# A windowed-attention and ternary-FFN layer: weight preparation moved from a stage of its own into the pipeline, and PV issued once per head group

## The chip, the cores and the metric

One core of a Trainium2 chip runs the kernel. The metric is the device time of one execution in microseconds.

## The reference

Input x is (8, 1024, 512) in fp32. Two sublayers follow each other, each with a layer norm ahead of it and one behind it, inside the residual:

```
x = x + layernorm(attn(layernorm(x)))
x = x + layernorm(ffn(layernorm(x)))

attn: q, k, v = x @ W.T + b; 16 heads of 32; blocks of 256 queries see the 256 keys
      up to and with their own; softmax; out @ Wo.T + bo
ffn:  h = x @ tern(w_fc).T + gate * (x @ v.T @ fast_b.T @ u.T)
      r = relu(h); out = (r * r) @ tern(w_proj).T
tern(w) = clip(round(w / s), -1, 1) * s,  s = mean(|w|) of each row (at least 1e-5)
```

w_fc is (2048, 512), w_proj (512, 2048), the four attention weights (512, 512), u (2048, 16), v (16, 512).

## The kernel before

All operands of products are split into an fp16 part and an fp16 rest (`product3` multiplies three of the four combinations), scaled by powers of two, so that an fp32-like result comes out of fp16 matmuls. The weights therefore need work before use: their largest absolute value (for the power of two), the two parts, a transpose; for the FFN the mean of absolute values of each row, a ternary value for every element, a transpose.

`build` runs two stages, each a block of its own with its own memory. **`prepare`** does all weight work: it loads Wq, Wk, Wv, Wo (1 MB each) and eight pieces of 1 MB of w_fc and w_proj, takes maxima on VectorE and across partitions with GpSimd's `partition_all_reduce`, splits on ScalarE and VectorE (L406, L471), sums absolute values on ScalarE (L422), makes the ternary values on VectorE (L493, L496), transposes everything 128 by 128 on TensorE (L377, L383, L390, L396), which VectorE and ScalarE copy out of PSUM (L350), and computes some 40 small constants on VectorE (L508 to L557).

**`steps`** then loops over 32 steps of 256 rows (4 a sequence, `t` the step, `p = t % 4` its place). Each step has 32 slots, one for each of 4 head groups x 2 query tiles x 4 heads, and five engines run the same slot program, written out by hand: tables such as `QK_SLOT` or `FF1_SLOT` say at which slot a piece of work is issued and lags (`LAG_T`, `LAG_PV`) how many slots a consumer comes after. `due(it, table, slot, lag, base)` gives the entries that fall on a slot, for the step `base` ahead of or behind the one whose scores are running. Projections are made one to two steps ahead, x is normalized two to three steps ahead, output projection and FFN run one to two steps behind; so the loop runs from -2 to 34. An engine goes through its items in order; a semaphore wait of one item holds all behind it.

In a step, scores S of a head are made on TensorE (L740), masked with a row maximum on VectorE (L1027), exponentiated on ScalarE for the row sum (L910); then the scores are made a second time transposed, T (L754), with the shift inside the product, exponentiated straight into `PT` (L924), masked on GpSimd (L1236, L1239), and multiplied with V on TensorE (L771, `Ob`): four heads of a group side by side in 128x32 column tiles, in fp32. `weighted_values` is called for each half (past keys, own keys) of a head group, two batches of 16 matmul records per group; a sequence's first step has only the second half. `PT` has 8 buffers.

SyncE's queue issues all DMAs: the loads of x, the transposes of the normalized x (`turn_x` L653, `turn_x2` L664, 128x1024 fp16 each), the transposes of the softmax shift (L676) and, for each head group, 12 DMAs that stack the parts of q and k on partitions (`stack`, L691). `qk32` has two buffers; the FFN's output tile `yc` is separate from the attention's `yb`.

## Time and profile before

| | us |
|---|---|
| median of 3 runs (2378.79 to 2380.89) | 2378.9 |
| profiled execution | 2378.28 |
| its span, first to last instruction | 2376.6 |
| TensorE busy in it | 2217.4 |
| VectorE busy | 1696.3 |
| ScalarE busy | 1643.4 |
| GpSimd busy | 1355.0 |

The span is that of one execution taken by the profiler; what lies around it is 1.7 us. "Busy" of TensorE counts from a matmul's start to its modelled end, and matmuls overlap. SPq is SyncE's queue, whose rows are the times it takes to issue DMAs. PEclk is the granted clock as a share of full speed. DMA share is the mean busy share of the 16 DMA engines.

### The profile page before, as it was taken

How to read it: one execution, taken by the hardware profiler on the slowest of the kernel's cores; microseconds unless marked ns; L12 is line 12 of the kernel's file. 1: busy time of each engine (PE TensorE's matmuls, PEld its weight loads, DVE VectorE, ACT ScalarE, POOL GpSimd, SP SyncE). 2: the span in 40 equal slices, each digit the busy share in tenths (PEclk: the TensorE clock that was granted, in tenths of full speed). 3: DMA queues.
4: the chain of work that ended last, by engine and by line, in shares of the span. 5: the costliest groups of instructions: out<-in, count | busy, mean ns of one | idle time of the engine just before them, and what ended most of it. 6: DMA issues, size and time to landing. Idle time of an engine off the chain costs nothing.

```text
span 2376.6 us, 60643 instructions
## 1 busy us (share of the span) xinstructions
PE 2217.4 (93%) x20124; PEld 1645.5 (69%) x20124; DVE 1696.3 (71%) x4247; ACT 1643.4 (69%) x4613; POOL 1355.0 (57%) x2473
## 2 busy tenths in 40 slices
PE   3267899999999999999999999999999999999998
PEld 2244677777777777777777777777777777777665
DVE  7535677777777777777777777777777777777754
ACT  4326777677767777677766777677776777677762
POOL 2023566566656666666665666665665666655553
PEclk9588999999999999999999999999999999999999
DMA  6112223322223222222222232232222322232210
GB/s 224 27 44 69 59 62 72 76 70 61 63 69 72 60 68 73 73 62 71 60 66 69 66 74 63 71 71 62 63 64 74 73 70 60 73 67 53 59 30 27
DMA packets 323336, 159.90 MB, mean 67 GB/s; under 512 B 203456, under 2 KB 293568, under 8 KB 322512
## 3 DMA queue, kind: packets, MB, share of 16 engines
q1 hardware_dynamic: 323024, 156.03, 26.7%
q8 instruction: 161, 2.64, 0.5%
q14 instruction: 151, 1.24, 0.2%
HBM read 46.83 MB, written 16.78 MB: 27 GB/s over the span
## 4 chain that ended last, share of the span: by engine, by line
PE 82%; SPq 5%; DMA 3%; ACT 2%; DVE 2%; issue 1%; POOL 0%; POOLq 0%; ACTq 0%; DVEq 0%
PE Ab L781 19%; PE F L836 19%; PE F L863 15%; PE Cb L781 9%; PE Ob L771 7%; PE Tb L754 6%; PE S L740 5%; SPq L691 5%; PE F L848 3%; DMA x2T<-xs 2%; DMA xT<-xs 1%; ACT PT L924 1%; ACT Sm L910 0%; DVE lnst L1044 0%; DVE Sm L1027 0%
## 5 line engine op out<-in xcount | busy, mean ns | idle before, releaser
L924 ACT ACTIVATE PT<-Tb 128x384 f32<-128x384 f32 x896 | 438.8, 490 | 418.9 <-PE Tb L754 413.7
L910 ACT ACTIVATE Sm<-Sm,nmax 128x384 f32<-128x384 f32 (+2 forms) x1024 | 584.2, 571 | 129.7 <-DVE nmax L1027 126.1
L1027 DVE CUSTOM_DVE_ANT_0 Sm<-S,mask,scales 128x384 f32<-128x384 f32 (+2 forms) x1024 | 572.2, 563 | 120.6 <-PE S L740 109.9
L836 PE MATMUL F<-x2T,t 128*128 128x256 f16 x4096 | 489.1, 272 | 0.0
L863 PE MATMUL F<-t,r 128*128 128x512 f16 x2048 | 483.5, 379 | 0.7 <-DVE r L1129 0.7
L836 PEld LDWEIGHTS F<-x2T,t 128*128 128x128 f16 x4096 | 397.9, 98 | 52.2
L781 PE MATMUL Ab<-xT,w_attn 128*128 128x256 f16 x3072 | 384.5, 276 | 37.0 <-DMA xT<-xs 32.3
L781 PEld LDWEIGHTS Ab<-xT,w_attn 128*128 128x128 f16 x3072 | 294.0, 99 | 95.5 <-issue 49.3
L1239 POOL TENSOR_SCALAR_AFFINE_SELECT PT<-PT 128x256 f32<-128x256 f32 x512 | 260.8, 513 | 173.5 <-ACT PT L924 172.7
L863 PEld LDWEIGHTS F<-t,r 128*128 128x128 f16 x2048 | 195.5, 98 | 201.0 <-ACT r L974 4.6
L740 PE MATMUL S<-QK 96*128 96x384 f16 (+2 forms) x1280 | 315.4, 280 | 10.3 <-DVE nmax L1027 10.3
L1256 POOL TENSOR_TENSOR sq<-r 128x512 f32<-128x512 f32 x256 | 272.5, 1064 | 81.1 <-ACT r L974 79.3
L754 PE MATMUL Tb<-QK 128*128 128x256 f16 (+1 forms) x1792 | 295.5, 247 | 23.5 <-ACT PT L924 21.5
L1208 POOL TENSOR_TENSOR lnrs<-lnve,nhalf 128x1 f32<-128x1 f32 x256 | 166.7, 651 | 173.8 <-DVE lnve L1099 60.3
L1236 POOL TENSOR_SCALAR_AFFINE_SELECT PT<-PT 128x256 f32<-128x256 f32 x384 | 184.9, 482 | 134.0 <-ACT PT L924 132.1
L754 PEld LDWEIGHTS Tb<-QK 128*128 128x128 f16 x1792 | 170.8, 98 | 102.3 <-ACT PT L924 28.7
L1129 DVE TENSOR_TENSOR r<-sq,r 128x512 f16<-128x512 f32 x256 | 188.5, 737 | 57.1 <-POOL sq L1256 29.3
L974 ACT ACTIVATE r<-F,c 128x256 f32<-128x256 f32 x512 | 211.8, 467 | 15.8 <-PE F L848 13.9
L1244 POOL TENSOR_TENSOR qkp<-qk,qkp 128x512 f16<-128x512 f32 x128 | 159.3, 1245 | 72.6 <-DVE qkp L1076 72.6
L781 PE MATMUL Ab<-w_attn,xT 128*128 128x256 f16 x1536 | 189.2, 273 | 9.5 <-ACT qk L948 9.5
L910 ACT ACTIVATION_READ_ACCUMULATOR Sm<-Sm,nmax 128x1 f32 x1024 | 197.9, 193 | 0.0
L771 PE MATMUL Ob<-PT,V 128*32 128x128 f32 (+1 forms) x3584 | 194.1, 334 | 0.0
(158 smaller groups left out, 3007.7 us busy)
## 6 DMA issues: line engine op xcount, KB each, us to landing
QK<-qkp SPq DMA_DIRECT2D x1536, 32.0 KB, 1.9
xa<-in_x SPq DMA_DIRECT2D x64, 256.0 KB, 2.9
x<-in_x SPq DMA_DIRECT2D x64, 256.0 KB, 3.0
out<-yc SPq DMA_DIRECT2D x64, 256.0 KB, 2.2
stage<-in_w_fc SPq DMA_DIRECT2D x4, 1024.0 KB, 9.2
stage<-in_w_proj SPq DMA_DIRECT2D x4, 1024.0 KB, 5.8
turned<-parts SPq DMA_TRANSPOSE x128, 2.3
stage<-in_Wq SPq DMA_DIRECT2D x1, 1024.0 KB, 5.5
```

Source lines behind the costliest of these rows:

```text
L740: mm = pe.matmul(Sb[j % 2][:, place * P:(place + n) * P], Q3[0:ST, h, qc * P:(qc + 1) * P], K3[0:ST, h, slot * P:(slot + n) * P], start=Tr ...
L754: mm = pe.matmul(Tb[:, col:col + width], K3[:, h, ring + key:ring + key + P], Q3[:, h, q0:q0 + width], start=True, stop=True, skip_group_c ...
L771: mm = pe.matmul(Ob[r * HD:(r + 1) * HD, q0:q0 + width], V[:, c, h * HD:(h + 1) * HD], src[:, blk * P:blk * P + width], start=(first and k ...
L781: mm = pe.matmul(outp, a(pa, k), b(pb, k), start=(n == 0), stop=(n == 3 * KD - 1), skip_group_check=True)
L836: pe.matmul(Fb[b][:, half * STEP:(half + 1) * STEP], W["t1"][:, k, mc * P:(mc + 1) * P], x2T[:, part, k, :], start=(half == 0 and k == 0 a ...
L863: mm = pe.matmul(o[:, :], r2[:, part, m, i * P:(i + 1) * P], W["t2"][:, m, :], start=(m == 0 and part == 0), stop=(m == KH - 1 and part == 1),
L910: act.activation(blk, blk, ACT.Exp, bias=nmax[:, hg % 2, j % 8:j % 8 + 1], scale=-1.0, accum_out=sums[:, hg % 2, j % 8:j % 8 + 1]).then_in ...
L924: act.activation(PT[:, n % NPT].rearrange("p b n -> p (b n)"), Tb[:, 0:WIN], ACT.Exp, bias=1.0, scale=c_score).then_inc(M["T_exp"], 1)
L974: ins = act.activation(r32[:, b, half * STEP:(half + 1) * STEP], Fb[b][:, half * STEP:(half + 1) * STEP], ACT.Relu, scale=W["c1"][:, 2 * m ...
L1027: v.tensor_tensor_reduce(Sm[:, j % NSM, c0:WIN], Sb[j % 2][:, c0:WIN], W["mask"][:, c0:WIN], W["c"][:, 3:4], 3e38, ALU.add, ALU.min, nmax[ ...
L1239: g.affine_select(out=blk, in_=blk, compare_op=ALU.is_ge, fill=zero, base=0, pattern=[[0, 2], [1, P]], channel_multiplier=-1).then_inc(M[" ...
L1256: g.tensor_tensor(sq32[:, m % 2], r32[:, m % 2], r32[:, m % 2], ALU.mult).then_inc(M["r2_sq"], 1)
```

## The change

`prepare` is gone; there is one block. What it did goes to three places.

At the head, ahead of the slot loop (`weights()` on each engine): loads of Wq and Wk, then x of step 0; their maxima, which no longer go through GpSimd: TensorE transposes the column of 128 partial maxima, broadcast, into PSUM (`turn_columns`), and VectorE reduces it (`read_columns`); the split; the transposes of Wq and Wk as DMAs from SyncE (four of 128x1024 each, `turn_weight`), then `turn_x` of step 0.

In the slots of the first steps, as items (`prologue(it, table, slot, lag)`, which counts slots from the loop's begin, 64 being the first slot of step 0): Wv at 24 and Wo at 44; the eight FFN pieces at 50, 58, ... 106, each over 12 slots (abs sums on ScalarE, comparison on GpSimd, ternary step on VectorE, DMA transposes by SyncE at lag 11: four of 128x512 for w_fc, one of 128x2048 for w_proj); the constants at 82 to 114. ScalarE's queue issues the loads of the pieces. Their buffers lie in tiles that the loop doesn't use yet.

In every step: `weighted_values` runs once for a head group with all four spans (32 records; 16 in a sequence's first step); `PT` has 12 buffers counted through all steps; `qk32` has one buffer; `yc` is `yb`.

```diff
+PIECES = 8
+WEIGHT_SLOT = {24: 2, 44: 3}
+PIECE_SLOT = {50 + 8 * n: n for n in range(PIECES)}
+PIECE_LOAD = {34: 2, 50: 3, 64: 4, 72: 5, 96: 6, 104: 7}
+CONST_SLOT = {82: 0, 85: 1, 87: 2, 88: 3, 89: 4, 90: 5, 112: 6, 114: 7}
...
+def prologue(it, table, slot, lag):
+    entry = table.get((it.t - BEGIN) * SLOTS + slot - lag)
+    if entry is not None:
+        yield entry
...
-        qk32 = sb("qk32", [P, 2, 2, STEP], F32)
+        qk32 = sb("qk32", [P, 2, STEP], F32)
-        NSM, NPT = 3, 8
+        NSM, NPT = 3, 12
-        yc = sb("yc", [P, TILES, D], F32)
+        yc = yb
...
+            def turn_weight(w):
+                sp.wait_ge(M["w_lo"], w + 1)
+                for c in range(KD):
+                    sp.dma_start(W["w"][:, w, :, :, c * P:(c + 1) * P].rearrange("p a k n -> p (a k) n"),
+                                 w_split[w][:, c].rearrange("p a i -> p (a i)"),
+                                 transpose=True).then_inc(M[f"w_turned{w}"], 16)
+            def turn_piece(n):
+                sp.wait_ge(M["f_tern"], n + 1)
+                if n < 4:
+                    for m in range(4):
+                        sp.dma_start(W["t1"][:, :, (4 * n + m) * P:(4 * n + m + 1) * P],
+                                     f_tern[n % 2][:, m * D:(m + 1) * D],
+                                     transpose=True).then_inc(M[f"f_turned{n % 2}"], 16)
+                else:
+                    sp.dma_start(W["t2"][:, :, (n - 4) * P:(n - 3) * P], f_tern[n % 2],
+                                 transpose=True).then_inc(M[f"f_turned{n % 2}"], 16)
...
+                    for w in prologue(it, WEIGHT_SLOT, s, 4):
+                        turn_weight(w)
+                    for n in prologue(it, PIECE_SLOT, s, 11):
+                        turn_piece(n)
...
+            def turn_columns(k, cols):
+                pe.wait_ge(M["col_max"], k + 1)
+                need(pe, M["max_read"], k)
+                for j, c in enumerate(cols):
+                    mm = pe.transpose(Fb[0][:, j * P:(j + 1) * P], c.to_broadcast([P, P]), idf)
+                mm.then_inc(M["turned_max"], 1)
...
-            def weighted_values(t, p, hg, half):
-                n = tile_of(p, 8 * hg + half * GROUP + GROUP - 1)[3]
-                pe.wait_ge(M["T_masked"], tiles_before(t, p) + n + 1)
+            def weighted_values(t, p, hg):
+                last = tile_of(p, 8 * hg + 2 * GROUP - 1)[3]
+                pe.wait_ge(M["T_masked"], tiles_before(t, p) + last + 1)
+                need(pe, M["OT_lo"], t * NGROUP + hg)
                 pe.wait_ge(M["A_free"], t * NA + V_POS[1] + 1)
+                now, past = p * TILES, (p - 1) * TILES
+                spans = [(now, 0, 0, STEP, 0), (now + 1, 2, P, P, 0)]
+                if p:
+                    spans = [(past + 1, 1, 0, STEP, GROUP), (past, 0, 0, P, GROUP)] + spans
...
-                    if ok and i % GROUP == GROUP - 1 and tile_of(p, i):
-                        weighted_values(t, p, i // 8, i // GROUP % 2)
+                    if ok and i % 8 == 7:
+                        weighted_values(t, p, i // 8)
...
+                weight_hi(0)
+                weight_hi(1)
+                for i in range(TILES):
+                    a_hi(0, i)
+                for n in range(2):
+                    act.wait_ge(M[f"w_turned{n}"], KD * 16)
+                    load_piece(n)
...
+            def output_max():
+                then(v.tensor_tensor(u_sc, u_in, u_in, ALU.mult))
+                then(v.tensor_reduce(usq, u_sc, AX.X, ALU.add))
+                v.tensor_reduce(red[:, 7:8], usq, AX.X, ALU.max)
+                weight_max(3, 6).then_inc(M["col_max"], 1)
```

## Rows read from the trace of the kernel before

**Rows 1.** Windows by stage: stretch, length, busy us (instructions) of each engine, PEclk, DMA share, GB/s.

```profile
0.00:116.00 116.00, 30.65 (x285) 27.64 (x286) 76.92 (x161) 50.11 (x71) 15.42 (x43) 0.71 0.38 125
116.00:139.60 23.60, 19.07 (x144) 14.62 (x144) 6.16 (x14) 3.04 (x8) 4.48 (x5) 0.90 0.05 19
139.60:180.80 41.20, 22.46 (x170) 17.36 (x170) 14.74 (x55) 15.23 (x54) 9.13 (x20) 0.83 0.27 66
180.80:229.90 49.10, 34.08 (x292) 23.16 (x292) 28.04 (x88) 33.42 (x107) 18.88 (x50) 0.86 0.25 60
229.90:293.40 63.50, 52.72 (x516) 39.05 (x514) 43.64 (x110) 44.59 (x129) 31.34 (x70) 0.95 0.27 64
...
363.20:2225.00 1861.80, 1853.51 (x16989) 1381.90 (x16987) 1392.01 (x3511) 1363.89 (x3899) 1155.76 (x2083) 1.00 0.28 67
```

**Rows 2.** Timeline of the weight stage: start us, us, engine, line, operation.

```profile
4.43 9.02 POOL L296 CAST QK<-ksel 32x512 f16<-32x512 f32 x16
6.31 2.29 DVE L449 TENSOR_REDUCE red<-stage 128x1 f32<-128x2048 f32 x1 [6.31 <-DMA stage<-in_Wq]
...
25.84 7.68 ACT L406 ACTIVATE s_hi<-stage,sW 128x2048 f16<-128x2048 f32 x4 [23.78 <-DVE sW L467]
27.88 6.88 DVE L471 SCALAR_TENSOR_TENSOR s_lo<-stage,sW,s_hi 128x2048 f16<-128x2048 f32 x3 [1.19 <-ACT s_hi L406]
...
57.25 0.62 ACT L422 ACTIVATE junk<-stage 128x512 f16<-128x512 f32 x1
59.16 1.67 DVE L493 TENSOR_SCALAR s_lo<-stage,h 128x512 f16<-128x512 f32 x4
60.87 2.74 DVE L496 SCALAR_TENSOR_TENSOR s_hi<-stage,h,s_lo 128x512 f16<-128x512 f32 x4
...
89.17 0.15 DVE L514 TENSOR_SCALAR bnd<-pow_out 128x1 f32<-128x1 f32 x1 [7.18 <-POOL pow_out L306]
...
96.07 0.91 DVE L557 COPY u_stack<-u_part 128x256 bf16<-128x256 bf16 x6
```

**Rows 3.** Timeline from the first x to the first projection.

```profile
108.06 5.93 SPq L653 DMA_TRANSPOSE xT<-xs  x2
...
115.94 5.15 PE L781 MATMUL Ab<-xT,w_attn 128*128 128x256 f16 x24 [16.91 <-DMA xT<-xs]
```

**Rows 4.** Timeline of SyncE's queue in the fill.

```profile
140.98 7.81 SPq L691 DMA_DIRECT2D QK<-qkp  x12
...
180.85 1.24 SPq L653 DMA_TRANSPOSE xT<-xs  x1
```

**Rows 5.** SyncE's waits, from 139.6 to 180.8, then from 180.8 to 229.9.

```profile
SPq L674 <- POOL parts L1228: 1.1, 1, 1.1
...
SPq L81 <- PE Tb L754: 4.7, 3, 2.6
SPq L81 <- POOL parts L1228: 3.3, 2, 2.1
```

**Rows 6.** Windows: weight loads, and the second xT transpose (columns as above).

```profile
20.00:40.00 20.00, 8.15 (x84) 7.79 (x85) 18.03 (x24) 13.80 (x17) 0.72 (x2) 1.00 0.75 276
...
113.80:115.94 2.14, 0.00 (x0) 0.03 (x1) 0.00 (x0) 0.00 (x0) 0.00 (x0) 0.50 0.78 153
```

**Rows 7.** Timeline of TensorE around one PV batch; PV's records from 363 to 2225.

```profile
1039.57 0.33 PE L754 MATMUL Tb<-QK 128*128 128x256 f16 x2
1039.74 0.33 PE L740 MATMUL S<-QK 96*128 96x384 f16 x1
1040.00 0.86 PE L771 MATMUL Ob<-PT,V 128*32 128x256 f32 x16
1040.79 0.39 PE L848 MATMUL F<-z,u_T 96*128 96x256 bf16 x2
...
L771 PE MATMUL Ob<-PT,V x3072: 272/326/404, 365.7 to 2221.0; 128*32 128x256 f32 x192
```

**Rows 8.** Timeline: GpSimd's rest of one head group, ScalarE's next write of qk32.

```profile
999.99 1.16 POOL L1244 TENSOR_TENSOR qkp<-qk,qkp 128x512 f16<-128x512 f32 x1 [0.88 <-DVE qkp L1076]
...
1006.31 0.46 ACT L946 ACTIVATE qk<-Ab,bqs 128x256 f32<-128x256 f32 x1
```

More of the change, by code:

```diff
@@ new lines, in steps, with carve @@
+        f_raw = [w_raw[n] if n in (2, 3) else r2w.bitcast(F32)[:, n % 2 * 4 * D:(n % 2 + 1) * 4 * D] for n in range(PIECES)]
+        f_junk = V[:, 6:8].rearrange("p c d -> p (c d)").bitcast(F16)
+        f_below = r32[:].rearrange("p a n -> p (a n)").bitcast(F16)
+        f_tern = [sq32[:].rearrange("p a n -> p (a n)").bitcast(F16), x2T[:].rearrange("p a k n -> p (a k n)")]
+        u_stack = V[:, 4:6].rearrange("p c d -> p (c d)").bitcast(BF16).rearrange("p (m c) -> p m c", m=KH)
+        def carve(tile, widths):
+            flat, at, out = tile, 0, []
+            for w in widths:
+                out.append(flat[:, at:at + w])
+                at += w
+            return out
@@ L724, in _, with weights, low_rank_weights, output_scales @@
         def _(pe):
+            def turn_columns(k, cols):
[4 more added lines that the diff above has]
+                mm.then_inc(M["turned_max"], 1)
+            def weights():
+                pe.wait_ge(M["pool_ready"], 2)
+                turn_columns(0, [red[:, 0:1]])
+                turn_columns(1, [red[:, c:c + 1] for c in range(1, 4)])
+            def low_rank_weights():
+                pe.wait_ge(M["fb6_done"], 1)
+                pe.wait_ge(M["max_read"], 4)
+                for k in range(KD):
+                    mm = pe.matmul(Fb[0][:, k * LR:(k + 1) * LR], v_in[:, k * P:(k + 1) * P], fb6, start=True, stop=True)
+                mm.then_inc(M["vp_full"], 1)
+            def output_scales():
+                pe.wait_ge(M["s2_ready"], 1)
+                pe.wait_ge(M["max_read"], 5)
+                for c in range(KD):
+                    mm = pe.transpose(Fb[0][:, c * P:(c + 1) * P], s2c[:, c:c + 1].to_broadcast([P, P]), idf)
+                mm.then_inc(M["s2_full"], 1)
             def scores(t, p, j):
@@ L892, in body @@
                         scores_transposed(t, p, i)
+            weights()
             run_iterations(pe, body)
@@ L1012, in body @@
                         z_second(t)
+            weights()
             run_iterations(act, body)
@@ L1198, in body @@
                         masked_scores(it.t, it.p, s)
+                    for w in prologue(it, WEIGHT_SLOT, s, 0):
+                        value_max() if w == 2 else output_max()
+                    for w in prologue(it, WEIGHT_SLOT, s, 1):
+                        value_scale() if w == 2 else output_scale()
+                    for w in prologue(it, WEIGHT_SLOT, s, 3):
+                        weight_lo(w)
+                    for n in prologue(it, PIECE_SLOT, s, 4):
+                        thresholds(n)
+                    for q in range(4):
+                        for n in prologue(it, PIECE_SLOT, s, 5 + q):
+                            ternary(n, q)
+                    for k in prologue(it, CONST_SLOT, s, 0):
+                        ffn_consts(k)
+            weights()
             run_iterations(v, body)
@@ L1290, in body @@
                             second_residual(t, p, i)
+            weights()
             run_iterations(g, body)
```

769 lines of the change are left out of this document (372 added, 397 removed).

## The prediction

> **What bounds the kernel now.** I read the execution by stages first, cutting it where SyncE issues the transpose of the next step's x [rows 1]. The last row of that group is the steady state: TensorE is busy 1853.5 of 1861.8 us, at full clock. Nothing taken from VectorE, ScalarE, GpSimd or the queues pays there; only TensorE's own time does. The first row is the opposite: `prepare` and the first x take 116 us with TensorE busy 30.7 us, and nothing in it is attention. The three rows after it are the fill of the pipeline: 23.6, 41.2 and 49.1 us, TensorE busy 19.1, 22.5 and 34.1 us. So I read those two places apart: what stands on the way to the first projection, and what paces the fill. In the fill that is SyncE's queue. Twelve stacking DMAs take 7.8 us to issue [rows 4], a step has 48 of them, and in the first 41.2 us stretch SyncE, once it has begun, waits only 1.1 us, in the next 4.7 + 3.3 = 8.0 us [rows 5]. In the steady state the same 30 us of issue hide under a step of some 68 us (1861.8 us hold 27.4 steps).
>
> Times below are sums against the profiled execution, 2378.28 us for a span of 2376.6; the median of the runs, 2378.9, lies 0.6 above.
>
> **The head.** Before, the first projection matmul starts at 115.94, behind three matters: all weight work (its last constants end at 97.0 [rows 2], two copies follow), then the load of x and its statistics, then its two transposes [rows 3]. After, only Wq and Wk stand in front. I walk the new chain on rows of the same shapes [rows 2]. Wq is there at 6.3; its maximum takes 2.29 (8.6). The transpose through TensorE and the read of 128 columns replace GpSimd's all-reduce; the trace has no such pair, so I take two semaphore hops and a small reduce, 1 us, between 0.5 and 2 (9.6). Three small VectorE operations of 0.2 give the scale (10.2). The fp16 part of a weight costs ScalarE 7.68/4 = 1.92, the rest 6.88/3 = 2.3 on VectorE. VectorE does in order: maximum of Wk (12.8), its columns and scale (15), statistics of x tile 0 (16), the rest of Wq (18.4), x again, the rest of Wk (22.5), x (25), constants (27). The 4.5 MB in front, at the 276 GB/s of a stretch full of such loads [rows 6], take some 16 us and are in by 18, when SyncE's queue is wanted for the first transpose.
>
> From 18.4 the DMA engines set the pace: four transposes of Wq, four of Wk, two of x, each of 128x1024 fp16 as the xT transpose of now. That one keeps the 16 engines 78% busy over 2.14 us, which is 1.67 us of all of them [rows 3, 6] and more than the 1.24 of its issue [rows 4]. Ten take 16.7, and 1.5 us pass before the first moves: 36.6. ScalarE starts the loads of two FFN pieces behind the transposes of Wq and Wk, 1 MB each, on the same engines; at 276 GB/s that is 3.8 us a piece, of which about one falls in front of x. First projection: 40, between 35 (loads hidden, everything as above) and 48 (both loads in front and the constants late). Change **-76** (-81 to -68).
>
> A page speaks about this rate. The Trainium skill ("DMA: Bandwidth & Descriptors", section "Latency and other measured facts") gives a DMA transpose 261 GB/s; 256 KB would then take 1.0 us, ten 10 us, and the head would be some 7 us shorter. The trace shows 256 KB in 1.67 us, which is 157 GB/s, and the sum above goes by that.
>
> **From there to the first stretch's cut** (23.6 us before). The projections of step 0 are TensorE's, 19.1 of 23.6 us, so what comes between counts. Wv's split and transposes run while the four Q/K halves do and just arrive (estimate 51 for a use at 51): nothing, up to 4 if late. Wo's maximum is a wait put into TensorE's order: the four column transposes stand between the halves of V tile 1 and the last Q/K group, and wait for VectorE's two 0.42 us passes over u and a 2.29 us maximum, 3.5 in all, less the half of V already queued: +3. Then SyncE waits for Wo's rest and issues its four transposes before x of step 1, 4 x 1.67 us of engine time in front of it: +5 on top of a cut that must in any case wait for the last projection (xT is one buffer). FFN pieces 2 and 3 loading beside it: +2. Together **+10** (5 to 18).
>
> **First filled stretch** (41.2 us before, SyncE without slack). Pieces 0, 1 and 2 are turned in it, four transposes each; twelve issues of 1.24 are 15, less the 1.1 us of wait and another 1 from the stacking rows that now wait less: **+13** (8 to 20). What the other engines get: four abs sums of 0.62 per piece on ScalarE (2.5 us); the ternary step, four of 0.69, on VectorE; the comparison on GpSimd, which the trace prices on VectorE at 0.42 and for a GpSimd pass of 512 elements at 9.02/16 = 0.56 [rows 2], so 2.2 us a piece, at most twice that. Three pieces are 8, 9 and 7 to 14 us on engines that are busy 15.2, 14.7 and 9.1 of 41.2 [rows 1]: covered.
>
> **Second filled stretch** (49.1 us before, 8.0 us of SyncE wait). Piece 3 (four issues), pieces 4 to 6 and u (one each, of 128x2048, twice the engine time of xT's): eight issues, 10 us, less 8: +2. The low-rank constants, which now run from 89.17 to 96.97 as one chain on VectorE [rows 2], fall into seven slots together with ternary steps; VectorE is busy 28.0 of 49.1 and gets 8 + 11 more, which fits over the stretch but not over those slots: +4. **+6** (0 to 18). The last piece and the s2 rows fall into a stretch of 63.5 us in which SyncE has room: nothing, up to 3. If this cover failed, late FFN weights would hold `turn_x2` of step 0 and SyncE behind it.
>
> **PV once per head group.** The matmuls are the same, the batches fewer: 4 x 7 x 8 = 224 become 128; 96 times an entry and an exit go. A batch of 16 records starts 0.26 after the S matmul before it, which itself streams 0.17 (T to S in the same rows), and the next operation starts 0.79 later [rows 7]. Four heads run side by side, so it streams twice 256 and twice 128 columns. A record lasts 0.272 at 128 columns and, half of them being twice as wide with the middle at 0.326, about 0.38 and at most 0.404 at 256; so 128 columns stream in 0.107 to 0.13, and six such units in some 0.64. So 0.26 - 0.17 + 0.79 - 0.64 = 0.24 us of a batch is entry and exit. 96 x 0.24 = 23; some of it falls into the fill, and a batch twice as long holds S and T back once, so I take **-20** (-23 to 0).
>
> The Trainium skill ("TensorE: Matmul & The Clock Gate", section "Measured speedup vs the span model") has packed tiles cost one matmul's time and about 4 ns a tile more. By that a batch has next to no entry of its own, and joining them saves at most a few us, not 20. The 0.24 us above is what this trace shows.
>
> **At nothing.** `qk32` with one buffer: ScalarE's next write must wait for GpSimd's rest of the group before; that one starts at 999.99, takes 1.16, and the next write starts at 1006.31 [rows 8]: 5 us of cover. If it went, TensorE would wait at Ab. `yc` in `yb`'s place: VectorE's own order puts the last read of yb tile 0 one slot ahead of the write, and the store leaves ten slots (20 us) before its reuse. PT's twelve buffers: a tile is reused two slots after its batch, as before. The end of the kernel is as it was.
>
> **Sum:** -76 + 10 + 13 + 6 - 20 = -67, thus 2311; I add 3 for small waits in the third stretch: **2314**.
>
> **Rivals.**
> 1. Forecast, 2314, own range 2300 to 2330: chance 0.58.
> 2. The items choke the fill: VectorE and ScalarE, not SyncE, become its pace because the items come in bursts and in an in-order queue. Each of the two stretches then takes its high end and the head its high end: -68 + 18 + 20 + 18 - 20 = -32: 2346. For: a slot of the fill lasts 1.3 to 1.5 us and an item adds 0.8 to it on each of three engines, with waits from one to the other. Against: the busy times above. 0.14.
> 3. Joining PV saves nothing, because TensorE then waits for T's exponentials, or because the 0.24 us isn't paid per batch: 2334. Against: TensorE's records are gapless otherwise. 0.14. The span model of the Trainium skill named above would end here too.
> 4. Transposes queued back to back go at the pace of their issue, 1.24 instead of 1.67 us: ten are 4.3 us shorter, 2310, and perhaps a little more from Wo's and the pieces': 2307. Against: 256 KB were never moved faster than in the row. 0.06. The Trainium skill's rate for DMA transposes leads to the same place.
> 5. Slower than before: the joined batch stalls TensorE at every group, all steps long, since it needs the masks of eight tiles and holds S and T. All but PV gives -47; over 128 groups that is used up at 0.37 us each. At 0.5 it would be 2378 - 47 + 64 = 2395. For: it is the only edit that acts in the steady state, where all counts. Against: the second half batch already waited for the same last mask at the same lag. 0.04.
> 6. The change doesn't do what it says: FFN weights come so late that the head only moves, and step 0's FFN waits for what was saved: around 2378. Against: the last piece is turned ten slots before its first use. 0.04.
>
> The range reaches from just below case 4 to part of case 2: 2294 to 2342. A change under 0.2% (4.8 us) can't be told from none here. Faster 0.94 (cases 1 to 4 and part of 6), same 0.02, slower 0.04.
>
> **What would show it.** The first projection near 40, ten transposes before it back to back; the three cuts 34, 54 and 55 us apart instead of 23.6, 41.2 and 49.1; SyncE without wait in the first two; 32 records per PV batch with one gap at either side, and the step time in the steady state 0.7 us lower in three of four. Wrong: the first projection later than 50; an FFN wait of TensorE in step 0; waits of ScalarE at `qk` or VectorE at `yb` in every step.

## The result

The changed kernel takes **2346.68 us** (median of four runs, 2345.23 to 2347.89) against 2378.85 for the kernel before, measured beside it: a ratio of 0.9865, 95% interval 0.9848 to 0.9882. The sign was right, the forecast of 2314.0 was 33 us too low, and the range, which ended at 2342.0, missed the time by 4.7 us. The profiled run took 2345.23 us for a span of 2343.5.

Windows of the changed kernel, cut as [rows 1] were, with the columns of that group: the head, then from the first projection on to the cuts where SyncE issues the transpose of the next step's x, and the steady state.

```profile
0.00:54.00 54.00, 9.47 (x54) 6.50 (x54) 25.41 (x51) 10.22 (x10) 19.48 (x39) 0.99 0.88 236
54.00:82.50 28.50, 14.07 (x98) 10.45 (x98) 11.33 (x21) 5.42 (x10) 2.98 (x3) 0.80 0.25 65
82.50:138.30 55.80, 27.58 (x177) 19.19 (x177) 30.32 (x81) 25.49 (x86) 33.29 (x33) 0.74 0.46 120
138.30:208.20 69.90, 42.18 (x300) 26.79 (x301) 52.41 (x158) 41.77 (x133) 47.94 (x68) 0.74 0.47 110
208.20:274.00 65.80, 55.45 (x514) 41.17 (x513) 44.53 (x112) 44.79 (x129) 33.00 (x73) 0.87 0.31 69
...
343.60:2192.00 1848.40, 1836.76 (x16988) 1388.22 (x16986) 1385.96 (x3512) 1365.77 (x3900) 1165.37 (x2084) 1.00 0.27 68
```

And the timeline rows that set the cuts (the first is TensorE's first projection):

```profile
41.73 4.66 PE L540 MATMUL Ab<-xT,w_attn 128*128 128x256 f16 x24 [11.50 <-DMA xT<-V]
...
82.55 1.25 SPq L313 DMA_TRANSPOSE xT<-xs  x1
...
138.29 1.24 SPq L313 DMA_TRANSPOSE xT<-xs  x1
...
208.19 1.24 SPq L313 DMA_TRANSPOSE xT<-xs  x1
...
274.00 1.24 SPq L313 DMA_TRANSPOSE xT<-xs  x1
```

With the same rows of before (115.94, 139.64, 180.85, 229.87, 293.37) every term of the prediction's sum gets its measured size:

| stretch | before | after | change | predicted |
|---|---|---|---|---|
| start to the first projection | 115.9 | 41.7 | -74.2 | -76 |
| to the first cut | 23.7 | 40.8 | +17.1 | +10 (5 to 18) |
| first filled stretch | 41.2 | 55.7 | +14.6 | +13 (8 to 20) |
| second | 49.0 | 69.9 | +20.9 | +6 (0 to 18) |
| third | 63.5 | 65.8 | +2.3 | +3 |
| the rest, to the end | 2083.2 | 2069.5 | -13.7 | -20 (-23 to 0) |
| span | 2376.6 | 2343.5 | -33.1 | -64 |

The head came close to its working. Three terms did not: the way to the first cut (7 us), the second filled stretch (15 us) and PV (6 us). Stretches are read from one profiled execution of each kernel and scatter more than the medians do: over the fifteen kernels of this document that join PV "the rest" lies between 2069.3 and 2074.9, and the changed kernel's 2069.5 is at its low end, so PV's gain by this reading is 8 to 14 us. In the windows the second stretch has VectorE busy 52.4 us where it was 28.0 before, GpSimd 47.9 for 18.9, and TensorE's granted clock at 0.74 for 0.86; yet the busiest of them, VectorE, fills only three quarters of it. The experiments ask what set its length.

**PV.** TensorE's timeline around one joined batch of a steady step; the matmul behind it starts where the next row does:

```profile
1108.91 0.33 PE L496 MATMUL S<-QK 96*128 96x128 f16 x2
1109.17 1.51 PE L530 MATMUL Ob<-PT,V 128*32 128x256 f32 x32
1110.61 0.61 PE L540 MATMUL Ab<-xT,w_attn 128*128 128x256 f16 x4
```

From the last start of S to the next operation are 0.26 + 1.44 = 1.70 us for 32 records. Two batches of 16 took, by [rows 7], 2 x (0.26 + 0.79) less one S matmul of 0.17, that is 1.93. A joined batch saves 0.23 us, as the prediction's 0.24 had it.

**What SyncE did.** Its waits in the first and second filled stretch:

```profile
SPq L340 <- DVE sq L991: 1.0, 1, 1.0
SPq L87 <- POOL parts L1325: 0.2, 1, 0.2
...
SPq L87 <- POOL parts L1325: 7.0, 2, 4.0
SPq L87 <- PE Tb L512: 3.6, 2, 3.4
SPq L423 <- DVE V L1040: 3.4, 1, 3.4
```

In the first it waits 1.2 us of 55.8: there the queue is full, as forecast. In the second it waits 14.0 us, against 8.0 before [rows 5], and half of that for the row sums at the end of the attention work. The prediction had these waits used up by eight more issues; they grew instead. So the second stretch isn't SyncE's.

### The profile page after: what moved, and what is told of

It is laid out like the page before. It is cut to its first block, busy times and chain, and to the rows that moved or that the text cites. A ratio compares the mean times of both kernels' runs of the same rounds, so it can differ in the third digit from the quotient of the medians.

```text
span 2343.5 us, 60162 instructions
## 1 busy us (share of the span) xinstructions
PE 2188.6 (93%) x19862; PEld 1635.4 (70%) x19862; DVE 1685.0 (72%) x4242; ACT 1626.6 (69%) x4613; POOL 1422.9 (61%) x2499
## 4 chain that ended last, share of the span: by engine, by line
PE 74%; DVE 8%; SPq 6%; issue 4%; ACT 3%; DMA 2%; POOL 1%; ACTq 0%; DVEq 0%; POOLq 0%
PE Ab L540 18%; PE F L608 17%; PE F L635 11%; PE Cb L540 9%; PE Ob L530 6%; PE Tb L512 6%; PE S L496 5%; SPq L401 3%; PE F L620 2%; DVE lnst L1073 1%; DMA x2T<-xs 1%; DVE QK L1065 1%; DVE yb L1124 1%; SPq L331 1%; ACT Sm L731 1%
## 5 line engine op out<-in xcount | busy, mean ns | idle before, releaser
L540 PE MATMUL Ab<-xT,w_attn 128*128 128x256 f16 x3072 | 385.4, 276 | 40.8 <-DMA xT<-xs 23.7
L1336 POOL TENSOR_SCALAR_AFFINE_SELECT PT<-PT 128x256 f32<-128x256 f32 x512 | 267.2, 527 | 111.3 <-ACT PT L750 107.6
L1257 POOL TENSOR_TENSOR lnrs<-lnve,nhalf 128x1 f32<-128x1 f32 x256 | 174.8, 683 | 165.0 <-DVE lnve L1131 60.2
L1333 POOL TENSOR_SCALAR_AFFINE_SELECT PT<-PT 128x256 f32<-128x256 f32 x384 | 186.3, 485 | 129.1 <-ACT PT L750 127.4
L1161 DVE TENSOR_TENSOR r<-sq,r 128x512 f16<-128x512 f32 x256 | 188.7, 738 | 56.5 <-POOL sq L1353 28.8
L540 PE MATMUL Ab<-w_attn,xT 128*128 128x256 f16 x1536 | 199.5, 282 | 19.7 <-ACT qk L776 14.7
L1314 POOL TENSOR_TENSOR shift_c<-sums,isum 128x8 f32<-128x8 f32 x128 | 28.6, 223 | 284.8 <-ACT isum L739 284.8
```

Of the source, the lines that this page charges most:

```text
L540: mm = pe.matmul(outp, a(pa, k), b(pb, k), start=(n == 0), stop=(n == 3 * KD - 1), skip_group_check=True)
L1161: v.tensor_tensor(lo, sq32[:, m % 2], hi, ALU.subtract).then_inc(M["r2_lo"], 1)
L1336: g.affine_select(out=blk, in_=blk, compare_op=ALU.is_ge, fill=zero, base=0, pattern=[[0, 2], [1, P]], channel_multiplier=-1).then_inc(M[" ...
```

## The experiments

Each is the changed kernel with one edit unless it says otherwise. Medians of four runs; the ratio is to the kernel before, measured beside each (2378.66 to 2378.99). "Lengths" are the stretches of the table above, from the first projection: to the first cut, first, second and third filled stretch (changed kernel: 40.8, 55.7, 69.9, 65.8). Ten kernels leave the way to the first cut as it is (the changed one; comparison moved or left out, single transposes, PV halves, constants, sooner loads; the three with added work). They reach it after 38.1 to 42.4 us, so 4 us of that length come and go by themselves. In the kernels whose edit leaves them alone, the first filled stretch takes 55.6 to 56.5 us, the second 69.5 to 69.9.

### The comparison on VectorE, and left out

The comparison of the ternary step was priced at 0.56 us, twice that at most. The groups of the changed kernel say (count, busy us, mean ns, idle before):

```profile
L1266 POOL TENSOR_SCALAR r<-r,yb 128x512 f16<-128x512 f32 x24 | 38.9, 1629 | 22.0 <-DVE yb L981 22.0
L1266 POOL TENSOR_SCALAR r<-t,yb 128x512 f16<-128x512 f32 x8 | 12.4, 1562 | 4.6 <-DVE yb L981 4.6
```

That is 1.6 us each, 51 us in all. The first kernel does the comparison on VectorE in front of each ternary operation; the second leaves it out, so that its FFN weights aren't the ternary ones.

```diff
-                    for q in range(4):
-                        for n in prologue(it, PIECE_SLOT, s, 4 + q):
-                            below(n, q)
...
+                v.tensor_scalar(f_below[:, cols], f_raw[n][:, cols], h[:, 0, c:c + 1], None,
+                                ALU.is_lt).then_inc(M["f_below"], 1)
                 v.wait_ge(M["f_below"], 4 * n + q + 1)
```

> The changed kernel with the FFN pieces' comparison (32 operations of 128x512, 1.56 us each on GpSimd in the trace after) moved to VectorE, where the same shape took 0.42 us. Theory G (GpSimd's comparisons pace the two filled stretches, because VectorE's ternary step waits for each and masks and q/k rests queue behind them): 15 to 25 us faster than the changed kernel, 2322 to 2332, both stretches shorter. Theory S (SyncE's transposes pace them): at most 3 us, 2344 to 2347. Theory V (VectorE is the pace, with its constants): slower by up to 10 us, since VectorE gets 13 us more.

> The changed kernel with the comparison left out altogether (the ternary step subtracts the raw weight in its place, so FFN values are not the reference's). It bounds what the comparison can cost wherever it runs. G: 18 to 28 us faster than the changed kernel, a few us more than with VectorE doing it. S: at most 3. V: as with the comparison on GpSimd.

On VectorE: **2341.10** (2340.73 to 2342.15), 0.9840 [0.9823, 0.9856]; lengths 42.1, 55.6, 66.1, 65.4. Left out: **2339.59** (2339.11 to 2342.40), 0.9838 [0.9822, 0.9854]; lengths 40.0, 55.3, 65.3, 65.9. The same operation costs VectorE 0.51 us (groups of the first kernel):

```profile
L990 DVE TENSOR_SCALAR r<-r,yb 128x512 f16<-128x512 f32 x24 | 12.3, 511 | 0.0
```

GpSimd loses some 22 to 26 us of work in each of the two stretches (33.3 to 10.7 and 47.9 to 21.9 us by the windows), and the first gets no shorter, the second by 3.8 to 4.6. So the whole comparison, at 1.6 us apiece on GpSimd, is worth 5.6 to 7.1 us of the time, not more: theory G, with its 15 to 28, is out, and S and V, which allowed no gain of this size, don't hold either.

The two kernels also price VectorE's time. Their windows of the first and second stretch, with the comparison on VectorE, then left out:

```profile
83.60:139.20 55.60, 27.12 (x181) 19.58 (x182) 36.42 (x103) 25.82 (x87) 10.73 (x21) 0.78 0.46 120
139.20:205.30 66.10, 39.55 (x291) 24.76 (x289) 53.78 (x166) 40.60 (x128) 21.85 (x50) 0.74 0.48 116
```

```profile
81.70:137.00 55.30, 29.39 (x176) 20.67 (x177) 26.47 (x81) 22.71 (x77) 9.77 (x18) 0.69 0.47 120
137.00:202.30 65.30, 40.64 (x296) 26.11 (x297) 49.65 (x161) 43.37 (x140) 22.36 (x52) 0.75 0.52 118
```

VectorE has 10.0 and 4.1 us less to do in the second kernel, 14.1 together, and the stretches are 0.3 and 0.8 us shorter, 1.1 together, no more than their scatter. And while GpSimd does the comparison, VectorE's own ternary operations take longer: 32 of them 29.8 us in the changed kernel, 24.8 with the comparison on VectorE.

### ScalarE's second load, and the loads beside the transposes

The chain from the first projection to the first cut in the changed kernel, timeline:

```profile
26.48 10.19 ACTq L712 DMA_DIRECT2D r<-in_w_fc  x2
...
31.10 0.17 DVE L889 RECIPROCAL yb<-yb 128x1 f32<-128x1 f32 x1
...
38.66 2.00 ACT L687 ACTIVATE PT<-t,yb 128x2048 f16<-128x2048 f32 x1 [14.17 <-issue]
...
54.05 5.30 PE L540 MATMUL Ab<-w_attn,xT 128*128 128x256 f16 x24 [3.92 <-DMA w_attn<-PT]
...
69.79 2.00 ACT L687 ACTIVATE PT<-t,yb 128x2048 f16<-128x2048 f32 x1 [5.89 <-DVE yb L889]
...
74.21 0.37 ACTq L712 DMA_DIRECT2D t<-in_w_fc  x1
74.21 8.24 SPq L331 DMA_TRANSPOSE w_attn<-PT  x4
```

Wv's scale is ready at 31.3, and its split starts at 38.66, for ScalarE goes through its items in order: it first waits for Wk's transposes so as to start the second FFN load, done at 36.67, and then loads three registers. And both `load_piece(2)` and `(3)` wait for the same semaphore as the transposes of Wv and Wo, `w_lo`; a load of 1 MB and four transposes start at the same instant. Two kernels: the second load as an item at slot 30; loads 2 and 3 behind the transposes.

```diff
-                for n in range(2):
-                    act.wait_ge(M[f"w_turned{n}"], KD * 16)
-                    load_piece(n)
+                act.wait_ge(M["w_turned0"], KD * 16)
+                load_piece(0)
...
+                if n == 1:
+                    act.wait_ge(M["w_turned1"], KD * 16)
```

> The changed kernel, but ScalarE doesn't wait for Wk's transposes and load FFN piece 1 before it splits Wv; that wait and load come at count 30, after the split. In the trace after, Wv's scale is ready at 31.2 and its split starts at 38.66. Theory A (this order makes V's first tile late): V's projection starts at its place right behind the second q/k group, some 5 us earlier, Wo's chain and everything behind it too: 5 to 8 us faster than the changed kernel. Rival (the cut waits for the transposes of Wo, whose time is set by the DMA engines): at most 2 us.

**2341.47** (2339.46 to 2344.93), 0.9839 [0.9823, 0.9856]; lengths 35.2, 55.8, 69.6, 67.2. The first cut comes 5.6 us sooner after the first projection, and the median is 5.2 lower, at the low end of theory A's 5 to 8.

```diff
                 if n in (2, 3):
-                    act.wait_ge(M["w_lo"], n + 1)
+                    act.wait_ge(M[f"w_turned{n}"], KD * 16)
...
-PIECE_LOAD = {34: 2, 50: 3,
+PIECE_LOAD = {46: 2, 60: 3,
```

> The changed kernel with the loads of FFN pieces 2 and 3 behind the transposes of Wv and Wo (ScalarE waits for these before it issues them, at counts 46 and 60) instead of starting with them. In the trace after, the load of piece 3 and the first of Wo's transposes are issued at the same 74.21, SyncE's queue is held for 8.2 us by four transposes instead of 5.2, and the 16 engines are full until 84. Theory D (the loads hold the transposes on the shared engines): x of step 1 is turned 4 to 7 us earlier after the first projection, 4 to 7 us faster than the changed kernel. Rival (the loads only move, and the sums of their pieces wait): within 2 us.

**2339.53** (2337.90 to 2340.81), 0.9836 [0.9819, 0.9852]; lengths 32.2, 55.8, 69.5, 65.9. Wo's transposes now hold SyncE's queue 5.3 us instead of 8.2 and begin 5.8 us earlier (timeline):

```profile
68.37 5.30 SPq L331 DMA_TRANSPOSE w_attn<-PT  x4
73.78 1.25 SPq L313 DMA_TRANSPOSE xT<-xs  x1
```

The two edits remove the same wait, and with it a fall of TensorE's clock. In the changed kernel TensorE stands idle for 3.92 us before V's first tile, until Wv's transposes have landed, and then its 24 matmuls take 5.30 us, at a granted clock of 0.51 (window 54.05 to 59.35), the lower of the two levels. In either kernel of this section V starts at its place, with 0.97 us ahead of it, and takes 2.78 at full clock. The kernel with single transposes (next section) has the wait and not the fall, and reaches the cut in 38.1 us instead of 40.8 (timeline):

```profile
52.86 2.79 PE L538 MATMUL Ab<-w_attn,xT 128*128 128x256 f16 x24 [3.90 <-DMA w_attn<-PT]
```

So here is the +17.1 of the second term: some 3 us of it are the wait for Wv's transposes, which either edit takes away, 2.5 the clock behind it, which falls in some kernels and not in others, and 2.9 the load beside Wo's transposes, which only the second edit takes away. With both edits the way takes 32.7 us (below), no less than with the second alone; the 8.5 to 9 us that it is still longer than before are the size of the forecast's other two terms, Wo's maximum and Wo's transposes (+3 and +5).

### One transpose for a w_fc piece

`t1` is laid out so that a piece is one transpose of 128x2048 instead of four of 128x512 (`turn_piece`), 12 issues fewer.

```diff
-                    for m in range(4):
-                        sp.dma_start(W["t1"][:, :, (4 * n + m) * P:(4 * n + m + 1) * P],
-                                     f_tern[n % 2][:, m * D:(m + 1) * D],
-                                     transpose=True).then_inc(M[f"f_turned{n % 2}"], 16)
+                    sp.dma_start(W["t1"][:, 4 * n * KD * P:4 * (n + 1) * KD * P].rearrange("p (c n) -> p c n", n=P),
+                                 f_tern[n % 2], transpose=True).then_inc(M[f"f_turned{n % 2}"], 16)
```

> The changed kernel with t1 laid out so that each w_fc piece is turned by one DMA of 128x2048 instead of four of 128x512: 12 issues of 1.3 us fewer on SyncE (15.6 us), same bytes. S (SyncE's issues pace the filled stretches): 10 to 15 us faster than the changed kernel. G: 0 to 4 us.

**2340.83** (2340.20 to 2341.49), 0.9840 [0.9824, 0.9857]; lengths 38.1, 51.2, 70.1, 65.5. The three pieces turned in the first stretch hold SyncE 1.7, 3.2 and 1.7 us instead of 5.2 each, which frees 9 us; the stretch gets 4.5 shorter, the second, where a fourth piece is turned, not at all. That is what the waits said: SyncE counts in the first stretch alone, and even there at half its price. The median gained 5.9 us, between theory S and theory G; some 2.7 of the profiled run's gain is the clock on the way to the first cut (the section above).

### PV in two batches again

```diff
+                    if p and half != k // 2:
+                        continue
...
-                    if ok and i % 8 == 7:
-                        weighted_values(t, p, i // 8)
+                    if ok and i % GROUP == GROUP - 1 and tile_of(p, i):
+                        weighted_values(t, p, i // 8, i // GROUP % 2)
```

> The changed kernel with PV issued in two batches per head group again, at the slots where the kernel before issued them; twelve PT buffers, one qk32 buffer and yc in yb's place stay. It measures the joining alone. Theory P (entry and exit of a batch, 0.2 to 0.24 us, are paid on TensorE's path): 96 more of them, 13 to 23 us slower than the changed kernel, 2360 to 2369, with the same fill. Rival (the 14 us that the steps after the fill lost come from the other edits): 2345 to 2350.

**2355.92** (2352.66 to 2359.99), 0.9900 [0.9883, 0.9916]; lengths 42.4, 56.4, 69.9, 66.4: 9.2 us more in the median, less than the 13 to 23 of theory P. In its profiled run, the slowest of its four, there are 12.5 more behind the fourth cut (2082.0 for 2069.5), where it stands as the kernel before did (2083.2). It has the twelve PT buffers, the single `qk32` and `yc` in `yb`'s place, so these three together cost next to nothing there. The batch is again that of [rows 7]:

```profile
1040.16 0.33 PE L496 MATMUL S<-QK 96*128 96x384 f16 x1
1040.41 0.86 PE L533 MATMUL Ob<-PT,V 128*32 128x256 f32 x16
1041.20 0.50 PE L544 MATMUL Ab<-xT,w_attn 128*128 128x256 f16 x3
```

Joining is the cause of the gain in the steady state. It is smaller than 96 x 0.23 = 22. In a window with the same number of matmuls ([rows 1] and the last row of after, 16989 and 16988) TensorE is busy 16.75 us less, and idle 11.6 us for 8.3: 3.3 come back as waits. One wait of TensorE in that window grew, for the softmax shift that VectorE writes into `QK` for T:

```profile
PE Tb L512 <- DVE QK L1065: 5.8, 21, 0.9
```

It was 0.6 us, once, before, and in the kernel with halves it is 0.6 again: the longer batch brings it. The window holds 27 of 32 steps, so about 82 of the 96 joins; 16.75/82 is 0.20 each. The others lie mostly in the fill, where TensorE isn't the bound.

### Later constants, sooner loads

The forecast put the second stretch's cost partly on the low-rank constants, which fall into seven slots with ternary steps. One kernel spreads them; another starts the last two FFN loads four slots sooner, since ScalarE waits 3.8 us for them.

```diff
-CONST_SLOT = {82: 0, 85: 1, 87: 2, 88: 3, 89: 4, 90: 5, 112: 6, 114: 7}
+CONST_SLOT = {79: 0, 82: 1, 85: 2, 88: 3, 91: 4, 95: 5, 112: 6, 114: 7}
...
-PIECE_LOAD = {34: 2, 50: 3, 64: 4, 72: 5, 96: 6, 104: 7}
+PIECE_LOAD = {34: 2, 50: 3, 64: 4, 72: 5, 92: 6, 100: 7}
```

> The changed kernel with the constants' items at counts 79, 82, 85, 88, 91, 95 instead of 82, 85, 87, 88, 89, 90. In the trace after, VectorE is a closed chain from 147.7 to 159.3 in the second stretch, SyncE waits 3.4 us for its last link (u), and four step-0 stackings queue behind. Theory V (the burst holds S and SyncE): 4 to 8 us faster than the changed kernel, all in the second stretch. Rival (the same work costs the same wherever it lies on an in-order engine): within 2 us.

> The changed kernel with the loads of FFN pieces 6 and 7 issued at counts 92 and 100 instead of 96 and 104; their sums come at 98 and 106. In the trace after, ScalarE waits up to 3.2 us for such a load in the second stretch, and the chain shows 4.9 us of it. Theory L: 3 to 6 us faster than the changed kernel. Rival: the wait on the piece two before moves to ScalarE instead, within 1.5 us.

Spread: **2345.59** (2340.41 to 2347.59), 0.9859 [0.9843, 0.9875]; second stretch 68.0. Sooner: **2345.54** (2343.71 to 2349.95), 0.9866 [0.9849, 0.9882]; second stretch 70.6. Neither can be told from the changed kernel, as both rivals had it. In the second kernel ScalarE's 3.8 us of waits for loads are gone from the second stretch, and its waits for VectorE's maxima have grown from 11.5 to 17.1: a wait that the table of waits names can be taken away and another takes its place.

### Together, and the work of each engine made dearer

> Three of the edits at once: comparison on VectorE, load of piece 1 behind Wv's split, w_fc pieces turned by one DMA each; alone they gave 5.6, 5.2 and 5.9 us. If the stalls follow each other on one chain (theory C: the fill is a chain of hand-offs between in-order queues, with no engine as its pace), the gains add to 14 to 18 us: 2329 to 2333. If they all draw on the same slack (one pacing resource behind them), 2337 to 2341.

The comparison on VectorE, the later second load and the single transposes together: **2334.85** (2333.19 to 2336.88), 0.9814 [0.9797, 0.9830]; lengths 36.1, 51.6, 68.6, 65.4. Alone they gave 5.6, 5.2 and 5.9 us, 16.7 in sum; together 11.8, between the two theories. The way to the first cut and the first stretch keep their gains; the second stretch, 66.1 with the comparison on VectorE alone, is back at 68.6.

If one engine paced the second stretch, its work would count fully and that of the others not at all. So three kernels add work in the two stretches: each ternary operation of VectorE done twice, each abs sum of ScalarE twice, and four 512-column matmuls of TensorE into a spare bank in each slot.

```diff
+                then(v.scalar_tensor_tensor(f_tern[n % 2][:, cols], f_raw[n][:, cols], h[:, 1, c:c + 1],
+                                            f_below[:, cols], ALU.is_gt, ALU.subtract))
...
+                act.activation(f_junk[:, q * D:(q + 1) * D], f_raw[n][:, q * D:(q + 1) * D],
+                               ACT.Abs).then_inc(M["act_step"], 1)
+                act.wait_ge(M["act_step"], 4 * n + q + 1)
...
+                    if 50 <= (it.t - BEGIN) * SLOTS + s < 114:
+                        for _ in range(4):
+                            pe.matmul(Fb[1][:, :], fill[:, 0:P], fill[:, 0:512], start=True, stop=True,
+                                      skip_group_check=True)
```

> The changed kernel with each ternary operation on VectorE done twice (same result): 32 more of 0.69 us and a wait for the first, some 0.8 us each, 12 to 13 us more VectorE work in each filled stretch. Its slope says how far VectorE paces the fill. Theory V (VectorE, 52.4 of 69.9 us busy in the second stretch, is its pace): that stretch grows by 10 to 13 us, the first, 30.3 of 55.8 busy, by less than 5; in all 12 to 18 us slower than the changed kernel. Theory C (hand-offs between in-order queues, no single pace): a third to a half of the added time in either stretch, 8 to 12 us in all. If neither, under 4.

> The changed kernel with each abs sum on ScalarE done twice: 32 more of 0.62 us and a wait, some 0.7 us each, 11 us more in each stretch on an engine busy 25.5 of 55.8 and 41.8 of 69.9 us. V: under 5 us in all. C: a third to a half, 7 to 11 us in all.

> The changed kernel with four dummy matmuls of 128x512 (bf16, 0.21 us each at full clock) into an unused bank at the head of each slot from count 50 to 113, so that TensorE's granted clock, 0.74 in both filled stretches after against 0.83 and 0.86 before, stays higher. It adds 0.86 us a slot, 27 us a stretch, where TensorE had 28 us idle. Theory K (the lower clock lengthens every TensorE hop of the fill, 42.2 us busy instead of 34.1 for the same work): clock above 0.9 and the two stretches together unchanged or shorter in spite of the added work, -6 to +6 us. Rival (TensorE's clock lies off the path): the added work shows where it stands in front of S and T, 10 to 30 us slower.

Windows of the two stretches, VectorE's work doubled, then ScalarE's, then TensorE's filled up:

```profile
82.30:143.00 60.70, 28.30 (x177) 19.17 (x177) 41.55 (x96) 25.70 (x87) 36.64 (x33) 0.75 0.44 110
143.00:219.00 76.00, 43.83 (x283) 26.45 (x284) 63.13 (x172) 40.36 (x128) 53.67 (x69) 0.68 0.41 102
```

```profile
81.30:138.70 57.40, 28.89 (x177) 19.89 (x177) 31.03 (x81) 34.13 (x99) 33.34 (x33) 0.73 0.47 116
138.70:210.40 71.70, 42.33 (x287) 26.25 (x288) 53.22 (x157) 50.50 (x147) 47.52 (x68) 0.72 0.51 107
```

```profile
82.00:141.40 59.40, 43.28 (x273) 26.86 (x273) 31.66 (x85) 25.83 (x87) 34.75 (x36) 0.88 0.46 113
141.40:211.10 69.70, 59.66 (x420) 36.09 (x421) 51.66 (x155) 42.35 (x131) 46.39 (x64) 0.93 0.45 110
```

| doubled | us | ratio | work added, 1st / 2nd | length added, 1st / 2nd |
|---|---|---|---|---|
| VectorE | 2358.07 | 0.9914 [0.9897, 0.9930] | 11.2 / 10.7 | 5.0 / 6.1 |
| ScalarE | 2350.22 | 0.9883 [0.9866, 0.9900] | 8.6 / 8.7 | 1.6 / 1.8 |
| TensorE | 2349.77 | 0.9874 [0.9855, 0.9893] | 15.7 / 17.5 | 3.6 / -0.2 |

VectorE's added work counts by 0.45 and 0.57, ScalarE's by 0.2 (lengths little above the scatter), GpSimd's (taken away, above) by up to 0.18, SyncE's by half in the first stretch and nothing in the second. By the medians VectorE's doubling lies inside theory C's 8 to 12 us (11.4), ScalarE's (3.5) below C's 7 to 11 and where theory V had it. TensorE's added matmuls made the two stretches 3.4 us longer, within theory K's -6 to +6. TensorE's is free in the second stretch, at 60 us busy of 70: its low clock costs nothing there that I can see, since the clock rose from 0.74 to 0.93 with the added matmuls, and the length stayed. (Extra time and faster own work may also cancel; one kernel doesn't part them.)

A share belongs to the kernel in which it was taken, not to the engine. The doubled ternary operations stand behind GpSimd's slow comparison; with that comparison gone from GpSimd, VectorE doing it or nobody is 14.1 us of VectorE's time and counted 1.1, that is by 0.08. Why the two differ so was not tried. No engine's work counts fully, so none of them alone is the pace. That the pace is the way through all their queues is what is left, and the shares fit it; no run shows it directly.

### All edits

The next takes the three of before with the spread constants and the sooner loads; the one behind it adds the loads behind the transposes; the last divides the comparison between VectorE (first and third quarter of a piece) and GpSimd.

> Comparison on VectorE, load of piece 1 behind Wv's split, w_fc pieces turned by one DMA each, loads of pieces 6 and 7 sooner, constants spread. The first three gave 11.8 us together, the last two 1 us each alone. If VectorE's burst and the loads come to matter once the others are gone: 2326 to 2331. If not: 2332 to 2336.

> The five edits and the loads behind the transposes. D, and gains that follow each other on one chain: 3 to 6 us faster than the five, 2324 to 2327. If not, 2328 to 2331.

> As the six together, but of each piece's four comparisons two stay on GpSimd, two go to VectorE. Theory V (with all four, VectorE paces the second stretch): that stretch 1 to 4 us shorter, 1 to 4 us faster than the six. Rival (each hand-off between the two costs what it saves): same or up to 3 us slower.

| | us | ratio | lengths |
|---|---|---|---|
| five edits | 2329.74 (2328.28 to 2331.61) | 0.9797 [0.9781, 0.9813] | 35.1, 50.2, 62.2, 66.4 |
| six | 2326.24 (2322.20 to 2330.51) | 0.9782 [0.9764, 0.9800] | 32.7, 50.8, 61.4, 65.5 |
| six, comparison divided | 2325.94 (2323.83 to 2328.68) | 0.9784 [0.9768, 0.9801] | 32.2, 50.7, 60.6, 65.7 |

Constants and loads, worth some 1 us each when alone, bring 5.1 here, in the profiled runs nearly all of it in the second stretch (62.2 for 68.6); which of the two does it wasn't tried. It is what the first case of the expectation had: they come to matter once the others are gone. The sixth edit, worth 7.2 alone, adds 3.5, inside the spread of the runs and of the 3 to 6 that theory D gave it. The last two are the fastest kernels of this study, 52 us below the kernel before and 20 below the changed one; they can't be told apart. The second stretch of the six edits, then with the comparison divided:

```profile
126.30:187.70 61.40, 40.07 (x294) 25.31 (x292) 57.47 (x175) 43.53 (x140) 24.31 (x51) 0.78 0.63 124
```

```profile
124.30:184.90 60.60, 39.75 (x294) 25.11 (x293) 53.16 (x164) 43.27 (x140) 35.67 (x59) 0.76 0.54 126
```

VectorE is busy 57.5 of 61.4 in the one; 4.3 us less work on it in the other, with 11.4 more on GpSimd, gives 0.8. Even at 94% it isn't shown to be the pace.

## Why the prediction was wrong

The place of the gain, its size in the head and the place of the loss were right. These steps stood or fell:

- **The head, -76: right.** -74.2. Ten transposes ran back to back; eight of them held the queue 14.65 us (from 19.54), where the sum by engine time said 1.67 each, 13.4 for eight. The working adds up to 36.6 and about 1 for the loads, 37.6; the 40 holds 2.4 us for which it gives no row. The first projection came 4.8 us after the last transpose was issued (36.92), so that part of the hit is luck.
- **To the first cut, +10: too small**, +17.1, still inside its bounds. The failed sentence is "Wv's split and transposes ... just arrive". I followed SyncE and the DMA engines there, and not ScalarE's order, in which the second load's wait stands ahead of Wv's split. TensorE waited 3 us more for them than the 0.97 between two such tiles, and lost another 2.5 to the lower clock, for which the sum had no term. "FFN pieces 2 and 3 loading beside it: +2" is 2.9 at Wo's transposes. Both causes were undone: 40.8 to 35.2 and to 32.2 us.
- **First filled stretch, +13: right** in size, +14.6, and SyncE without slack there (1.2 us of wait). But 9 us of its issues are worth only 4.5 when taken away, and 11 us of VectorE's work cost 5, so it is less purely SyncE's than I wrote.
- **Second filled stretch, +6 (0 to 18): wrong**, +20.9. This is the step that put the time out of the range. It failed in four places. The comparison was sized at 0.56 us (0.42 on VectorE) and takes 1.6; that part is worth 3.8 to 4.6 us. VectorE got 24.4 us more work, not 19, in part because its ternary operations take 0.93 us beside GpSimd's comparison, not 0.69. And the sentence "which fits over the stretch" takes busy sums for cover: there, doubled ternary operations cost 0.57 of themselves although VectorE was busy 75%. The sum's own term for SyncE, eight issues less 8 us of wait, didn't hold either: the waits grew to 14.0, and fewer issues gained nothing. By the measured shares GpSimd's 29 us more (x 0.18) and ScalarE's 8.4 (x 0.2) are some 7 of the 20.9 us, and VectorE's 24.4 are 2 to 14, by its share of 0.08 or 0.57: an estimate of 9 to 21, too wide to close the account.
- **The way it costs.** The chain of work through that stretch has no line of the kernel over 12% ("issue", where an engine waits for nothing that the profile shows, has 17.7). Its shares, and some pieces from it (start, length, what):

```profile
by line: issue 17.7%; SPq L401 11.3%; POOL r L1266 9.6%; DMA r<-in_w_proj 7.0%; PE Ab L540 5.8%; DMA turned<-parts 5.6%; DVE sq L991 4.2%; DVE Sm L1056 3.9%; SPq L344 3.4%; SPq L423 2.8%; ACT PT L750 2.0%; SPq L303 1.9%; ACT Sm L731 1.3%; D
...
145.99 1.57 POOL r L1266
147.67 0.64 DVE sq L991
...
158.56 0.77 DVE V L1040 x5
159.35 1.97 SPq L423
...
162.83 2.41 SPq L344
...
173.82 3.90 DMA turned<-parts
...
184.37 4.89 DMA r<-in_w_proj
190.78 2.74 PE Ab L540 x12
```

  It goes from GpSimd's comparison to the ternary step, through the constants to u's transposes on SyncE, the piece's transpose, the stacking, then over a weight load to the projections. The items' chains are hung between those of the attention. That each queue hands its delay on to the next is how I read this chain.
- **Third stretch, +3: right**, +2.3.
- **PV, -20: right in kind, too large**, -13.7. The 0.24 us of entry and exit was 0.23. Not all joins are paid: the filled stretches of the kernel with halves are no longer than the changed kernel's beyond scatter (56.4 and 69.9), and 3.3 us return as TensorE's waits, which the prediction named but took for the step from 23 to 20. Of the 13.7 up to 5 may be scatter; the medians say 9.2.
- **At nothing: right.** The kernel with halves keeps `qk32`, `yc` and PT's buffers and takes 2082.0 us for the rest, where the kernel before took 2083.2. None was tested by itself.

Rival 2, the items choking the fill, had chance 0.14 and the time 2346; the result is 2346.7. Its time was right by luck, its mechanism by half. Its terms were -68, +18, +20, +18 and -20 and came as -74.2, +17.1, +14.6, +20.9 and -13.7: three of them were too high, by 12.5 us together, PV's and the second stretch's too low, with the third stretch's 2.3 by 11.5. And it had VectorE and ScalarE as the pace, where the doubled works show neither to be it. What it had right is that items in in-order queues cost more than busy times say. Rivals 3 to 6 are out: joining saves, the eight transposes took 14.65 us, longer than by either of the two paces that rival 4 set against each other, nothing stalled the steady state beyond the 3.3 us above, and no wait for FFN weights stands in TensorE's table.

The Trainium skill ("TensorE: Matmul & The Clock Gate", section "Measured speedup vs the span model") has one matmul's time and some 4 ns a tile, and no term for the entry of a batch. The halves kernel, 9.2 us slower in the median, decides against summing by that formula alone for the 128x32 batches here.

**Open:** with all six edits the second stretch is still 12 us above the 49.0 of before (61.4), and how these divide between VectorE's work and the hand-offs isn't settled. Nor is it whether the low clock of TensorE costs anything in the first filled stretch, as it does on the way to the first cut.

## What to carry to other kernels

Work moved into the fill of a pipeline isn't covered because the busy sums fit: in in-order queues that hand to each other, added work on an engine that was busy three quarters of the time or less cost about half of itself in one kernel and a tenth in another, and two mended waits that brought 1 us each alone brought 5 beside three other edits. Price an operation on the engine that will run it, and follow every in-order queue past the moved step, the loads' issuing engine too. Don't let a bulk load and a transpose on the critical path wait for one semaphore: put the load behind.

## What the runs showed of the hardware

- **GpSimd's comparison.** `is_lt` of 128x512, fp32 to fp16, took 1.6 us on GpSimd and 0.51 on VectorE; GpSimd's cast of 512 elements on 32 partitions takes 0.56 [rows 2]. The Trainium skill ("GPSIMD Engine Reference", section "4.1 Engine selection") has one-input operations there "roughly line-rate"; here this one takes three times as long as on VectorE.
- **Transposes beside a load.** Four transposes of 128x1024 held SyncE's queue 5.3 us alone and 8.2 beside a load of 1 MB that another engine issued. The Trainium skill ("DMA: Bandwidth & Descriptors", section "Issuing engines are not separate DMA queues") says that both run on the same 16 engines and interleave; the trace agrees, at 2.9 us for this load.
- **A power on GpSimd at the start.** The first two `rstd`, 128x1, took 2.51 and 2.60 us (timeline of the first):

```profile
16.40 2.51 POOL L1257 TENSOR_TENSOR lnrs<-lnve,nhalf 128x1 f32<-128x1 f32 x1 [3.80 <-DVE lnve L1082]
```

  The third took 0.55, and the mean over all 256 is 0.68. Why was not tried.
- **The clock in the fill.** With TensorE busy 42.2 of 69.9 us the granted clock was 0.74, with 59.7 of 69.7 it was 0.93, and the stretch took the same time. On the way to the first cut, after the same idle time of 3.9 us, 24 matmuls took 5.30 us at a granted clock of 0.51 in one kernel and 2.79 at 1.00 in another, and there the difference reached the cut.
